# Path attention: the turn of the inverted blocks moves from ScalarE to VectorE, two row steps move past the logits, and the inverses load in another order

## What is computed

```python
Mw = where(strict, einsum('bhtd,bhsd->bhts', wh, wh) * bh, 0)
rhs = where(strict, einsum('bhtd,bhjd->bhtj', wh, kh) * bh, 0)
Bmat = solve_triangular(Mw + eye(t), rhs, lower=True)
qk = einsum('bhid,bhjd->bhij', qh, kh)
qw = where(incl, einsum('bhid,bhtd->bhit', qh, wh), 0)
logits = where(incl, (qk - einsum('bhit,bhtj->bhij', qw, Bmat)) * SCALE, -1e30)
o = einsum('bhij,bhjd->bhid', softmax(logits), vh)
```

## Time and profile before

| | |
|---|---|
| median of 3 runs | 2704.6 us (2700.51 to 2719.05) |
| the profiled execution | 2716.18 us, its span 2714.5 us |
| busy share of the span | PE 88%, its weight loads 62%, DVE 55%, ACT 34%, POOL 21% |
| mean granted clock of PE | 0.92 |
| path attention: projections | 2024 to 2150 us |
| path attention: first chunk and the 16 batches | 2150 to about 2490 us |
| in 2150 to 2490 | PE busy 298 of 340 us, DVE 240, POOL 179, ACT 132; granted clock 0.87 |

### The profile page before, as it was taken

How to read it: one execution, slowest core, us unless ns; L and a number is a source line. 1 busy time by engine, 2 the same in 40 slices (tenths; PEclk the granted TensorE clock), 3 DMA queues, 4 the chain that set the end, 5 groups by cost and what they waited for, 6 DMA issues and landing times. The chain is left out here.

```text
span 2714.5 us, 66840 instructions
## 1 busy us (share of the span) xinstructions
PE 2388.5 (88%) x29032; PEld 1694.1 (62%) x29032; DVE 1483.2 (55%) x2636; ACT 934.8 (34%) x1457; POOL 564.4 (21%) x589
## 2 busy tenths in 40 slices
PE   5999999999999988999888888878768589889698
PEld 2676766766676744555455555554443488888587
DVE  5234344344434343444599999965636467776400
ACT  2233333333333321111455555542117133334211
POOL 5930000000000000000132322323003265562200
PEclk9799999999999986899899999988889688889799
DMA  2000100010000000111333222201000222221130
GB/s 74 19 21 21 38 20 20 21 39 20 20 21 20 3 24 0 36 40 40 83 91 91 74 74 74 74 19 54 0 22 16 35 46 35 44 37 41 60 147 27
DMA packets 135940, 111.42 MB, mean 41 GB/s; under 512 B 109912, under 2 KB 121197, under 8 KB 130958
## 3 DMA queue, kind: packets, MB, share of 16 engines
q1 hardware_dynamic: 131342, 107.41, 15.1%
q10 hardware_dynamic: 4352, 0.26, 0.1%
HBM read 100.29 MB, written 7.34 MB: 40 GB/s over the span
## 5 line engine op out<-in xcount | busy, mean ns | idle before, releaser
L528 ACT ACTIVATE xa_probT<-psum,zero_column 128x1024 f32<-128x1024 f32 (+1 forms) x224 | 223.7, 1049 | 280.3 <-PE psum L376 280.3
L611 DVE COPY xa_v<-psum 128x512 f32<-128x512 f32 x96 | 66.4, 692 | 425.5 <-PE psum L353 425.5
L600 DVE TENSOR_REDUCE xa_part_max<-psum 128x2 f32<-128x802 f32 (+1 forms) x256 | 241.9, 987 | 60.5 <-PE psum L363 60.5
L353 PE MATMUL psum<-xa_wv,xa_ctxT 96*128 96x256 f32 (+1 forms) x832 | 215.8, 402 | 4.6 <-DVE xa_v L611 3.9
L374 PE MATMUL psum<-xa_qbd,xa_kT 32*128 32x128 f32 (+1 forms) x3328 | 218.8, 300 | 0.2
L345 PE MATMUL psum<-xa_ctxT,xa_wk 96*128 96x401 f32 (+1 forms) x512 | 209.1, 531 | 3.4 <-ACT xa_kT L521 1.4
L376 PE MATMUL psum<-xa_shift,xa_shift_of 32*128 32x128 f32 (+1 forms) x3328 | 208.7, 271 | 0.0
L374 PEld LDWEIGHTS psum<-xa_qbd,xa_kT 32*128 32x128 f32 (+1 forms) x3328 | 186.9, 180 | 15.3 <-issue 5.6
L1276 POOL TENSOR_TENSOR tk_exp_all<-tk_exp_all,tk_exp_left 128x577 f32<-128x577 f32 x64 | 121.0, 1890 | 354.7 <-ACT tk_exp_left L1397 354.7
L376 PEld LDWEIGHTS psum<-xa_shift,xa_shift_of 32*128 32x128 f32 (+1 forms) x3328 | 187.7, 183 | 0.0
L1444 DVE MAX8 tk_top<-tk_left 128x8 f32<-128x1601 f32 x96 | 175.1, 1824 | 4.1
(11 more groups left out here) (477 smaller groups left out, 4325.0 us busy)
## 6 DMA issues: line engine op xcount, KB each, us to landing
tk_ctx<-in_ctx SPq DMA_DIRECT2D x16, 1248.0 KB, 5.4
xa_ctxT<-in_ctxT SPq DMA_DIRECT2D x16, 1200.8 KB, 7.5
tk_ctxT<-in_ctxT SPq DMA_DIRECT2D x16, 1200.8 KB
ec_w<-in_ec_w SPq DMA_DIRECT2D x16, 1024.0 KB, 6.9
m_gate_up<-in_m_gate_up SPq DMA_DIRECT2D x17, 256.0 KB, 2.6
m_down<-in_m_down SPq DMA_DIRECT2D x17, 128.0 KB, 2.5
ff_w<-in_ff_w SPq DMA_DIRECT2D x2, 1024.0 KB
pa_minus_blocks<-pa_m_blocks SPq DMA_DIRECT2D x16, 128.0 KB, 2.2
```

The lines of the kernel that those rows point to most:

```text
L353: mm = mmul(ps[0:width(c), FILL, (c % 2) * D:(c % 2 + 1) * D], ctxT[:, h, k, c * P:c * P + width(c)], wv[:, k, :], start=(k == 0), stop=(k ...
L528: a_.activation(probT[0:w, par, u, :, 0:n], ps[0:w, at:at + 2, 0:n], ACT.Exp, bias=core.zero[0:w, :]).then_inc(e_done, 1)
L600: v.tensor_reduce(part_max[:, n, m, 2 * u:2 * u + 2], ps[:, at:at + 2, 0:z - a], AX.X, ALU.max, negate=True).then_inc(max_step, 1)
```

## The change

1. `turn_inverses` is now a DVE `tensor_copy` behind row step 15; ACT's one is removed, with its wait for `row_ready`.
2. In an even batch DVE now leaves two steps out of those in front of the logits: step 14 comes behind `log_out`/`masked_q`, and step 15, with the turn, in the next (odd) batch behind the additions of whole and ahead of its own seven steps. POOL's list is unchanged.
3. `store_inverses` stands in the odd batch's turn of SP's loop, ahead of its loads; in SP's queue this is the same place. The 8 loads of `inv` now all come ahead of the 8 of `invT`, and each kind has its own semaphore: x products wait for inv alone, the last update for invT.

```diff
--- before.py
+++ after.py
@@ -2079,6 +2079,7 @@
         level_ready = {n: sem(f"level_ready{n}") for n in (3, 4)}
         m_stored, m_loaded, v_stored, inv_loaded = ([sem(f"{n}{i}") for i in range(2)] for n in
             ("m_stored", "m_loaded", "v_stored", "inv_loaded"))
+        invT_loaded = [sem(f"invT_loaded{i}") for i in range(2)]
         terms_ready, row_ready, v_turned, started = sem("terms_ready"), sem("row_ready"), sem("v_turned"), sem("started")
         x_ps, x_sb, t_ps, t_done = (sem(n) for n in ("x_in_psum", "x_ready", "inv_in_psum", "inv_whole"))
         first_ps, first_sb, z_ps, z_sb, w_ps, sol_sb = (sem(n) for n in
@@ -2146,19 +2147,19 @@
                             sp.dma_start(dst[CH * c + u], src[:, c % 2, u].rearrange("p t c -> p (t c)")
                                          ).then_inc(v_stored[c % 2], 16)
 
-                def load_inverses(b, kinds=((inv, 0, inv_dram), (invT, T, invT_dram))):
+                def load_inverses(b, kinds=((inv, 0, inv_dram, inv_loaded), (invT, T, invT_dram, invT_loaded))):
                     c = b // CH
                     sp.wait_ge(v_stored[c % 2], 4 * 16 * (c // 2 + 1))
 
                     if b >= 2:
                         sp.wait_ge(t_done, G * (b - 1))
-                    for h in range(8):
-                        rows, cols = slice(S * h, S * h + S), slice(S * (h % 4), S * (h % 4) + S)
-                        for dst, by, src in kinds:
+                    for dst, by, src, loaded in kinds:
+                        for h in range(8):
+                            rows, cols = slice(S * h, S * h + S), slice(S * (h % 4), S * (h % 4) + S)
                             at = (S * h + by) % P
                             sp.dma_start(dst[at:at + S, b % 2].rearrange("p g j c -> p (g j) c")[:, :, cols],
                                          src[b, rows, :].rearrange("m (t c) -> t m c", t=S)
-                                         ).then_inc(inv_loaded[b % 2], 16)
+                                         ).then_inc(loaded[b % 2], 16)
 
 
                 for b in (0, 2, 3):
@@ -2167,17 +2168,17 @@
                         load_m(b // 2)
                 sp.wait_ge(zeroed, 2)
                 store_inverses(0)
-                load_inverses(0, ((inv, 0, inv_dram),))
+                load_inverses(0, ((inv, 0, inv_dram, inv_loaded),))
                 store_m(4)
                 for b in range(B):
+                    if b % 2 and b < B - 1:
+                        store_inverses((b + 1) // 2)
                     if b < B - 1:
                         load_inverses(b + 1)
                     if b + AHEAD < B:
                         store_m(b + AHEAD)
                         if (b + AHEAD) % 2:
                             load_m((b + AHEAD) // 2)
-                    if b % 2 == 0 and b // 2 + 1 < CHUNKS:
-                        store_inverses(b // 2 + 1)
 
             @block.gpsimd
             def _(pool):
@@ -2324,13 +2325,15 @@
 
                 def x_product(b, g):
                     if g == 0:
-                        pe.wait_ge(inv_loaded[b % 2], 16 * 16 * (b // 2 + 1))
+                        pe.wait_ge(inv_loaded[b % 2], 8 * 16 * (b // 2 + 1))
                         pe.wait_ge(level_ready[3], b + 1)
 
                     pe.wait_ge(rhs_raw, G * b + g + 1)
                     product(XB(b) + g, 4 * T, cTs[3][:, g], inv[:, b % 2, g], 1).then_inc(x_ps, 1)
 
                 def last_update(b, g):
+                    if g == 0:
+                        pe.wait_ge(invT_loaded[b % 2], 8 * 16 * (b // 2 + 1))
                     pe.wait_ge(x_sb, G * b + g + 1)
 
                     pe.wait_ge(qw_sb, G * b + g + 1)
@@ -2480,27 +2483,19 @@
                         act.wait_ge(k_ps, G * b + g + 1)
                         a.activation(flatter(rhs[:, g]), ps[:, at + g, 0:4 * T], ACT.Copy).then_inc(rhs_raw, 1)
 
-                def turn_inverses(c):
-                    act.wait_ge(row_ready, made_at(c, S - 1))
-                    if c >= 2:
-                        act.wait_ge(v_stored[c % 2], 4 * 16 * (c // 2))
-                    a.activation(blk_invT[:, c % 2], blk_inv[:, c % 2].rearrange("p b i j -> p b j i"), ACT.Copy
-                                 ).then_inc(v_turned, 1)
-
                 act.wait_ge(mt_sb, G * 2)
                 for h in range(8):
                     rows, cols = slice(S * h, S * h + S), slice(S * (h % 4), S * (h % 4) + S)
                     act.dma_start(m_dram[1, rows, :].rearrange("m (t c) -> t m c", t=S),
                                   mts[rows, 1].rearrange("p g j c -> p (g j) c")[:, :, cols]).then_inc(m_stored[1], 16)
                 right_out(0, XB(0))
-                turn_inverses(0)
                 act.wait_ge(zeroed, 2)
                 act.wait_ge(v_stored[0], 4 * 16)
                 for h in range(8):
                     rows, cols = slice(S * h, S * h + S), slice(S * (h % 4), S * (h % 4) + S)
                     at = (S * h + T) % P
                     act.dma_start(invT[at:at + S, 0].rearrange("p g j c -> p (g j) c")[:, :, cols],
-                                  invT_dram[0, rows, :].rearrange("m (t c) -> t m c", t=S)).then_inc(inv_loaded[0], 16)
+                                  invT_dram[0, rows, :].rearrange("m (t c) -> t m c", t=S)).then_inc(invT_loaded[0], 16)
                 for b in range(B):
                     for g in range(G):
                         act.wait_ge(x_ps, G * b + g + 1)
@@ -2519,8 +2514,6 @@
                         exponentials(b - 1)
                     if b < B - 1:
                         right_out(b + 1, YB(b))
-                    if b % 2 == 0 and b // 2 + 1 < CHUNKS:
-                        turn_inverses(b // 2 + 1)
                 at = YB(B - 1)
                 probs_turned(B - 2, at)
                 out_turned(B - 2, at)
@@ -2602,22 +2595,32 @@
                     masked_wb(b, XB(b))
                 for g in range(G):
                     masked_q(0, g, YB(0))
+                def turn_inverses(c):
+                    dve.wait_ge(row_ready, made_at(c, S - 1))
+                    v.tensor_copy(blk_invT[:, c % 2], blk_inv[:, c % 2].rearrange("p b i j -> p b j i")).then_inc(v_turned, 1)
+
                 def step(c, i):
                     if i <= OWN or c == 0:
                         multiply(c, i)
                     add_up(c, i)
+                    if i == S - 1:
+                        turn_inverses(c)
 
                 for i in range(1, S):
                     step(0, i)
                 for i in range(1, FIRST + 1):
                     step(1, i)
+                steps = []
                 for b in range(B):
-                    steps = steps_in(b)
+
+                    left, steps = steps, steps_in(b)
                     take = lambda count: [step(*steps.pop(0)) for _ in range(min(count, len(steps)))]
                     for g in range(G):
                         dve.wait_ge(t_ps, G * b + g + 1)
                         v.tensor_tensor(whole[:, g], in_bank(YB(b) + g, 0, 4 * T), invT[:, b % 2, g], ALU.add
                                         ).then_inc(t_done, 1)
+                    for s in left:
+                        step(*s)
                     take(7 if b % 2 else 2)
                     if b:
                         maxima(b - 1)
@@ -2634,11 +2637,13 @@
                         v.tensor_tensor(m, m, in_bank(YB(b) + g, 6 * T, 8 * T), ALU.add).then_inc(sol_sb, 1)
                     if b:
                         normalise(b - 1)
-                    take(len(steps))
+                    take(len(steps) - (0 if b % 2 else 2))
                     for g in range(G):
                         log_out(b, g)
                         if b < B - 1:
                             masked_q(b + 1, g, XB(b))
+                    if b % 2 == 0:
+                        take(1)
 
                 free, logs = YB(B - 1), XB(B - 1)
                 y_bank = (free + 3, logs, logs + 1, logs + 2, logs + 3, free + 3, logs, logs + 1)
```

## The result

The changed kernel takes 2719.8 us (median of 13 runs, 2713.1 to 2737.7), the kernel before 2705.2 (13 runs, 2694.4 to 2719.1): ratio 1.0065, 95% interval 1.0042 to 1.0087. It is slower, by 11 to 24 us; the forecast was no net change, 2703. The profiled executions took 2737.65 and 2716.18 us, so each stands at the high end of its own runs. Of the 21 us between them 8.6 lie ahead of the first x product (2165.8 us into the span before, 2174.4 after), a point that the sixteen profiles of this document reach anywhere between 2152 and 2174 us. The way from the first x product to that of batch 14 accounts for 6.6 us, batch 14 for another 4.0, and what follows for some 2.

The account below looks back on a forecast made before the run. Bound: PE's 22.5 us of waits for ACT's x in seven odd batches, and clock falls behind waits. Batch terms (+0.6, -0.5 twice each, +1.1, -2) and start (-0.3) gave about -1 on 2704.6: 2703, range 2684 to 2721.

Parts of the forecast that it names:

- ACT's x gone: Odd batches, PE's last update: the wait for ACT's copy of x goes, offering 4.9 us an odd batch.
- `first` held for POOL's `pa_rhs`: Odd batches, PE: `first` waits 2.3 us for the right sides masked by POOL, leaving 2.6 of the 4.9 gained.
- four products meet four POOL operations: Odd batches, DVE: one small product waits for each POOL operation (1.0, 1.0, 1.0, 1.3 us), the fourth done at 2277.2.
- the seven steps: DVE's small row steps (`take(7)`) in odd batches: expected to end at 2278.8 in batch 5, the same time as before.
- Batches 5 and 9: Odd batches with `queries` already late before: 0 with a clock fall, -4.7 us without; taken at -0.5 each.
- batch 1: Odd batch without spread_v, transposes and weighing: `queries` at about 16.7 us from the x products instead of 15.6, +1.1.
- batch 13: Odd batch with neither matrices nor the seven small steps: keeps what `first` gains, between 1.8 and 3.8 us; taken at -2.
- batches 3 and 7: Odd batches whose `queries` was not late before: between -0.3 and +4.4 us each with a clock fall; taken at +0.6 each.
- Zero, with at least 1 us to spare: Loads of inverses: last invT lands at 2287.1, batch 6 needs it at 2288 or later, so no cost.
- batch 11: Odd batch without matrices to form, its seven small steps staying: between -2 and +2 us, taken at 0.
- rival (b): Odd batches: DVE's chain ends later and the clock falls each time, 16 us slower, so 2721; chance 0.19.
- fifth collision: POOL's level operation behind z (1.28 us) against DVE's steps five to seven or shift; with a 1.1 us turn, up to +1.0.

Follow-up runs that it names:

- busy_q: Changed kernel with PE's product with the whole inverse (`second`) done twice in odd batches up to 11, ahead of the queries: ratio to the kernel before 1.0020.
- steps_act: Changed kernel with the turn back on ACT, behind its copies of x in the odd batch; moved steps and load order kept: ratio to the kernel before 1.0074.
- turn_only: Kernel before with only the turn changed to DVE's copy behind row 15, all row steps still in front of the logits: ratio to before 1.0016.
- loads_only: Kernel before with only the loads changed, eight of inv ahead of eight of invT, a semaphore for each kind: ratio to before 1.0005.
- small_after: Changed kernel with the seven small row steps of DVE's odd batches moved behind its masks of the matrices: ratio to the kernel before 1.0056.
- small_before: Kernel before with the seven small row steps of DVE's odd batches moved behind its masks of the matrices: ratio to before 1.0038.
- turn_reduce: Changed kernel with the turn written as a DVE tensor_reduce over an axis of one in place of tensor_copy: ratio to the kernel before 1.0051.
- spread: Changed kernel with step 14 back in the even batch and DVE's small steps dealt out to where DVE idles: ratio to the kernel before 1.0005.

## Why the prediction was wrong

**Right.** The waits that come and go, their places and sizes: ACT's x gone, `first` held for POOL's `pa_rhs` (2.3 us expected, 2.47 to 2.78 measured, seven times), at 7.0 us behind the x products (7.1). The turn stands behind `mask_right` and ends just behind it (2272.8 less 2265.3 = 7.5 us behind the x products; 7.4 measured), four products meet four POOL operations, and the seven steps end 13.6 us behind (13.5 worked out). What was said of the Trainium skill's "SBUF — State Buffer" (Who interferes with whom) the trace now bears out for a copy: 0.594 us for chunk 0, where POOL idles, 2.05 to 2.65 in the seven others. `queries` in batch 5: 18.1 expected, 17.5 measured. Batches 5 and 9: -0.5 expected, -0.4 and -0.2 measured; batch 1 +1.1 and +1.3; batch 13 -2 and -2.0. Batch 1 is in part luck: its `queries` came at 17.5 us and not at 16.7, and the way from there to the next x products was 0.6 us shorter than before.

**Wrong: batches 3 and 7.** The step that failed is in the sum: "batches 3 and 7 at the middle between fall and none ... I take +0.6 each". They measured +3.7 and +3.2. (+0.6 is not the middle either, which the prediction itself puts at +2.0: it was lowered because "a low clock behind the first wait brings PE to queries later and leaves the second wait short".) The part before it had named the case, "with a wait in front, and so with a fall of the clock that they did not have: between -0.3 and +4.4", and the earlier trace rows had shown that 0.85 us of wait is enough for a fall. The wait in after was 3.54 us in batch 3, where the clock did not fall behind the first wait, and 1.42 in batch 7, where it did, and the clock fell behind it in both, as in batches 1, 5 and 9. With rows that show a fall at 0.85 and a worked-out wait of 1.4 to 3.4, the fall was the likeliest, not the middle. What busy_q showed in its place: the clock behind the wait, some 4 us a batch, is the price, however short the wait was left.

**Wrong: batch 14.** "Zero, with at least 1 us to spare", but batch 13 was to be 2 us shorter, and the loads keep their time behind the turn; what batch 13 gained, batch 14 waited for, and the clock fell: 4.0 us. The margin was worked out for batch 6, whose batch 5 doesn't get shorter, and used for all. In steps_act, with the same order, batch 14 is 19.8 us too; in turn_only, which keeps the steps, 15.8.

**Wrong: batch 11.** Taken at 0 between -2 and +2; +2.4. It forms no matrices, but DVE's queue is as long, and the keys wait 2.21 us for `pa_sol`.

Put in, these make -1 + 2 x 2.9 + 4.0 + 2.4 = +11, the 10.6 us of the trace. (The prediction's own sum, -1 on 2704.6, is 2703.6.) The ratio says 11 to 24. The rest may be that before's own falls in batches 5 and 9 are not in every run: in loads_only's profile, with the same order, batch 7 falls and these two do not. In after each odd batch up to 11 falls. That fits, but nothing here counted falls over many runs, and it stays open.

The result is rival (b), with its end at 2721: each odd batch falls. It had a fifth collision and a turn of ACT's length as its cause; batch 5 shows neither. Its point of decision, some 0.9 us of wait in batches 3 and 7, was passed: 3.54 and 1.42.

## What to carry to other kernels

Where two engines take turns in holding a third, removing one wait moves it, unless the result that ends the stage comes earlier too: find that result (here DVE's masks, some 17.3 us behind the x products of batch 5 in five kernels) and shorten its own queue. Price a wait by what the clock does behind it, and take the fall as the likeliest when the trace has shown one at a shorter wait in the same place; a wait elsewhere in the batch may be longer and bring none. When a batch gets shorter, ask again of every transfer timed against it, batch by batch: the loads with 1 us to spare became the bound as soon as the odd batches were mended, and a second issuing queue then took the ratio from 1.0005 to 0.9940.

## What the runs showed of the hardware

- The granted clock can stay at 1.2 GHz long after the wait, with PE busy throughout: some 10 us in after, but 24 in batch 7 of busy_q (2304 to 2328), 20 in batch 1 of steps_act and 17 in batch 13 of small_after, each behind a wait of 2.5 to 2.8 us for the right sides. Batch 7 of busy_q takes 31.8 us by it, where its batches 5 and 9 take 22.8, and batch 13 of small_after 26.3, where that of after takes 20.2.
- The length of a wait does not settle whether the clock falls. Behind all 38 waits for `pa_minus_mt` in the batches of the sixteen traces, 0.84 to 6.29 us long, it fell. Behind 3.35 us for x (small_before, batch 3), 2.66 for the right sides (turn_reduce, batch 13) and 2.42 for `invT` (spread, batch 8) the granted clock stayed 1.00.
- One long wait can cost less than two short ones: 5.35 us in front of the last update (turn_only; batches 5, 7 and 9 take 24.2 to 25.3 us at a granted clock of 0.86 to 0.93), against 2.5 and 1.4 us in two places (the same batches of after: 26.3 to 26.5 us, 0.75 to 0.77).
- A DVE copy of 512 elements and a POOL operation shut each other out (0.594 us alone, 2.63 beside `mask_right`; POOL's q operation behind it takes 1.45 us where it takes 1.04 in turn_reduce); a reduction over an axis of length one, which does the same turn, doesn't wait (1.01 to 1.03 us in all eight).
- DVE's tiny products wait too, a whole POOL operation each: 0.78 to 1.03 us against 0.17 to 0.21.
- Eight small loads took 4.6 to 6.0 us to issue from SP and 4.5 from POOL; side by side on both, the last is issued 6.4 us behind the first instead of 10.6.
